# One attention layer on one core: scores and weighings joined into three stretches of TensorE's batch instead of five, products dealt between two PSUM banks, all orders rewritten

## The chip, the core and the metric

The kernel runs on one core of one Trainium2 chip. A core has TensorE (PE in the profile), VectorE (DVE), ScalarE (ACT), GpSimd (POOL) and SyncE (SP), which here issues all DMAs. The metric is the device time of one execution in microseconds (us); lower is better.

## The reference

For 32 batches of 256 rows and 384 columns: attention with 12 heads of 32 columns and an additive bias (`adj`, the same for all heads of a batch), an output product, a residual and a layer norm without gain.

```python
q = (x @ Wq.T).reshape(B, N, NUM_HEADS, HEAD)
k = (x @ Wk.T).reshape(B, N, NUM_HEADS, HEAD)
v = (x @ Wv.T + bv).reshape(B, N, NUM_HEADS, HEAD)
a = jnp.einsum('bnhd,bmhd->bhnm', q, k) * SCALE + encoding_bias[:, None, :, :]
pad_mask = jnp.all(a == 0, axis=-1)
a = jnp.where(pad_mask[..., None], -jnp.inf, a)
a = jax.nn.softmax(a, axis=-1)
o = jnp.einsum('bhnm,bmhd->bnhd', a, v).reshape(B, N, HIDDEN)
return o @ Wo.T + bo
x = _layernorm(x + _L0_gnn_ref(x, adj, ...), axis=-1)
```

## The kernel before

All is float32; products of full width are made of three matmuls of rounded parts (hi x hi, hi x lo, lo x hi). Every engine has its own program, written out by hand as `start()`, then `step(t)` for each of 27 batches (2 to 28), then `end()`. The loop over batches is a Python loop, so the program is unrolled. Engines wait for one another by semaphores; a wait inside an engine's program holds all that stands behind it.

One batch on TensorE. `project_kq` makes K and Q in three products, K01, K2Q0 and Q12, of 18 matmuls each (L779, 256 columns). `project_v` and `project_y` make v and the output in two halves of 9 matmuls each (V0, V1, Y0, Y1; L779, 384 columns). `scores(t, g)`, g = 0, 1, 2, makes the scores of four heads: 24 matmuls on tiles of 32 rows, four side by side (L828), into four banks, which the next group reuses after VectorE has read them. `weigh(t, g)` multiplies the exponentials of four heads with v: 16 matmuls on tiles of 32 columns, four side by side (L869). `transposes(t, u)`, u = 8 to 11, turns the exponentials of group 2 (L839). `spread` turns the inverse sums (L850), and `flag` makes one small product that tells whether a row of scores was all zero.

On VectorE `add_bias(t, u)` (L1185) adds the bias to the scores of two heads for half of the rows and takes their maximum: 12 units u of two heads, four in each group. ScalarE's `exps(t, u)` (L553) takes the exponentials into a ring of four units. The units of groups 0 and 1 are not turned by TensorE: VectorE's `square(t, u)` (L1202) turns their blocks of 32 x 32 into `sq_stage`, SyncE's `store_squares(t, g)` writes that 1 MB to a DRAM tensor (`sq_dram`, L250), and `load_squares(t, g)` reads it back in another order (`sq_probT`, L259). The read waits for the store's landing, and `weigh(t, g)` for the read's. SyncE issues DMAs one by one in its written order; a wait there holds all later ones. `load_bias_sq` and `load_bias` for batch c wait until all `add_bias` up to batch c - 2 are done.

ScalarE copies K and Q out of PSUM (`save_kq`), the turned exponentials (`copy_probT`), the weighed sums (`save_o`), rounds (`split_o_hi`) and normalises (`normalise`). VectorE adds `bv` (`save_v`, L1222), divides (`divide`), adds the residual (`residual`, L1285), takes `moments`, and reads the flag (`read_flag`, `mask`). GpSimd makes the lo parts (`split_xt`, `split_kq`, `split_o_lo`), `widen_inv`, `add_bo` and `deviation`.

PSUM has eight banks: four for scores, `bank_t` for the transposes, and `bank_a`, `bank_b`, `bank_c`. Before a product goes into one of these three, TensorE waits until the one before it in that bank was read, which the program writes as an explicit `pe.wait_ge` on `v_saved`, `kq_saved`, `y_saved`, `o_saved` or `o_n_ready`. Before the change `bank_b` holds K2Q0, Q12, V0, V1, Y0 and Y1, `bank_c` K01 and the spreads, and `bank_a` the weighed sums and the flag.

The order of TensorE in `step(t)` before: T11 of t-1, V1, K01 of t+1, Y0 of t-2, **W1 of t-1, S2**, K2Q0 of t+2, **W2 of t-1**, T8, Y1 of t-2, spread 0, flag, T9, **S0 of t+1**, Q12 of t+2, **W0**, T10, spread 1, V0 of t+1, **S1 of t+1** (W = `weigh`, S = `scores`, T = `transposes`; tiled stretches in bold).

## Time and profile before

| | us |
|---|---|
| median of three runs | 737.46 |
| profiled execution | 735.77 |
| its span, first to last instruction | 733.9 |
| span: start, 27 steps, end | 64.1, 592.4, 77.3 |

| engine | busy us | share of the span |
|---|---|---|
| TensorE, matmuls | 712.3 | 97% |
| TensorE, weight loads | 608.3 | 83% |
| VectorE | 588.5 | 80% |
| ScalarE | 616.7 | 84% |
| GpSimd | 453.0 | 62% |

The span leaves out 1.9 us of the profiled execution. 193 MB move by DMA at a mean of 263 GB/s; TensorE's granted clock is 0.996 of full in the mean. Busy time of TensorE is modelled and overlaps; where the text speaks of a stage's length, it is the time from the stage's first matmul to the next stage's first.

### The profile page before, as it was taken

How to read it: one execution, taken by the hardware profiler on the slowest of the kernel's cores; microseconds unless marked ns; L12 is line 12 of the kernel's file. 1: busy time of each engine (PE TensorE's matmuls, PEld its weight loads, DVE VectorE, ACT ScalarE, POOL GpSimd, SP SyncE). 2: the span in 40 equal slices, each digit the busy share in tenths (PEclk: the TensorE clock that was granted, in tenths of full speed). 3: DMA queues.
4: the chain of work that ended last, by engine and by line, in shares of the span. 5: the costliest groups of instructions: out<-in, count | busy, mean ns of one | idle time of the engine just before them, and what ended most of it. 6: DMA issues, size and time to landing. Idle time of an engine off the chain costs nothing.

```text
span 733.9 us, 23131 instructions
## 1 busy us (share of the span) xinstructions
PE 712.3 (97%) x7567; PEld 608.3 (83%) x7567; DVE 588.5 (80%) x2220; ACT 616.7 (84%) x1993; POOL 453.0 (62%) x516
## 2 busy tenths in 40 slices
PE   7999999999999999999999999999999999999985
PEld 7877888888888888888888888888888888888764
DVE  3886877888887898887798887888887788888873
ACT  4788888888888898888898888898888898888983
POOL 3674566675556675655676566676566676565362
PEclk9999999999999999999999999999999999999999
DMA  8468788878768888778778878878777868877782
GB/s 278 146 231 288 259 267 273 264 258 298 247 251 305 292 253 287 267 238 281 255 262 305 273 262 281 282 249 287 260 280 262 301 234 282 291 264 257 237 317 94
DMA packets 92712, 193.00 MB, mean 263 GB/s; under 512 B 4784, under 2 KB 51632, under 8 KB 84400
## 3 DMA queue, kind: packets, MB, share of 16 engines
q1 hardware_dynamic: 92592, 191.52, 76.9%
q8 instruction: 61, 1.00, 0.5%
q14 instruction: 59, 0.48, 0.2%
HBM read 111.80 MB, written 79.69 MB: 261 GB/s over the span
## 4 chain that ended last, share of the span: by engine, by line
PE 82%; DMA 9%; DVE 3%; POOL 3%; issue 2%; ACT 1%; DVEq 0%; SPq 0%; POOLq 0%; ACTq 0%
PE bank_b L779 41%; PE bank_a L869 11%; PE s_bank L828 10%; PE bank_c L779 8%; PE bank_t L839 8%; DMA sq_dram<-w_f 5%; DMA sq_probT<-sq_dram 3%; PE bank_c L850 2%; POOL kq_lo L400 1%; DVE neg L1185 1%; DVE w_f L1202 1%; DMA xt<-in_xT 0%; POOL kq_hi L398 0%; POOL xt_lo L389 0%; DVEq L1241 0%
## 5 line engine op out<-in xcount | busy, mean ns | idle before, releaser
L553 ACT ACTIVATE prob<-neg,negmax 128x256 f32<-128x256 f32 x768 | 380.6, 501 | 37.1 <-DVE negmax L1185 35.6
L1185 DVE CUSTOM_DVE_ANT_0 neg<-s_bank,bias_sq 128x256 f32<-128x256 f32 x512 | 190.3, 411 | 53.9 <-PE s_bank L828 43.8
L1202 DVE STREAM_TRANSPOSE w_f<-prob 128x512 f32<-128x512 f32 x256 | 173.1, 695 | 0.4 <-ACT prob L553 0.3
L553 ACT ACTIVATION_READ_ACCUMULATOR prob<-neg,negmax 128x1 f32 x768 | 147.8, 192 | 0.0
L400 POOL TENSOR_TENSOR kq_lo<-kq,kq_hi 128x512 fp32r<-128x512 f32 x96 | 125.4, 1306 | 7.7
L779 PE MATMUL bank_b<-xt_hi,w_hi 128*128 128x256 f32 x384 | 115.0, 300 | 0.9 <-POOL xt_lo L389 0.7
L779 PE MATMUL bank_b<-xt_lo,w_hi 128*128 128x256 f32 x384 | 108.6, 283 | 0.0
L779 PE MATMUL bank_b<-xt_hi,w_lo 128*128 128x256 f32 x384 | 108.3, 282 | 0.0
L1185 DVE CUSTOM_DVE_ANT_0 neg<-s_bank,bias 128x256 f32<-128x256 f32 x256 | 92.5, 416 | 10.8 <-PE s_bank L828 10.7
L426 POOL TENSOR_SCALAR var_eps<-meanvar 128x2 f32<-128x2 f32 x32 | 7.3, 228 | 142.7 <-DVE meanvar L1295 142.5
L410 POOL TENSOR_TENSOR o_lo<-o_n,o_hi 128x512 fp32r<-128x512 f32 (+1 forms) x62 | 61.9, 1020 | 38.7 <-ACT o_hi L578 38.6
L839 PE MATMUL bank_t<-ident,prob 128*128 128x128 f32 x512 | 82.9, 284 | 0.5 <-ACT probT L563 0.5
L436 POOL TENSOR_TENSOR xr<-xr,bo_all 128x768 f32<-128x768 f32 x32 | 59.1, 1849 | 38.0 <-DMA xr<-in_x 34.5
L779 PEld LDWEIGHTS bank_b<-xt_hi,w_hi 128*128 128x128 f32 x384 | 73.1, 190 | 8.8 <-DVE v L1222 1.0
L839 PEld LDWEIGHTS bank_t<-ident,prob 128*128 128x128 f32 x512 | 54.4, 141 | 29.2 <-issue 23.5
L563 ACT ACTIVATE probT<-bank_t 128x512 f32<-128x512 f32 x128 | 75.0, 586 | 2.3 <-PE bank_t L839 2.2
L398 POOL CAST kq_hi<-kq 128x512 fp32r<-128x512 f32 x96 | 58.9, 613 | 24.6 <-ACT kq L532 10.4
L779 PEld LDWEIGHTS bank_b<-xt_lo,w_hi 128*128 128x128 f32 x384 | 73.5, 191 | 0.0
L779 PEld LDWEIGHTS bank_b<-xt_hi,w_lo 128*128 128x128 f32 x384 | 73.5, 191 | 0.0
L779 PE MATMUL bank_b<-w_hi,xt_hi 128*128 128x384 f32 x192 | 70.7, 368 | 0.9 <-ACT kq L536 0.7
L869 PE MATMUL bank_a<-sq_probT,v 128*32 128x256 f32 x1008 | 68.3, 389 | 2.5 <-DMA sq_probT<-sq_dram 2.5
L828 PE MATMUL s_bank<-kq_hi 32*128 32x256 f32 x768 | 65.2, 328 | 1.8 <-POOL kq_lo L400 1.6
(83 smaller groups left out, 1779.4 us busy)
## 6 DMA issues: line engine op xcount, KB each, us to landing
sq_dram<-w_f SPq DMA_DIRECT2D x64, 1024.0 KB, 6.3
sq_probT<-sq_dram SPq DMA_DIRECT2D x64, 1024.0 KB, 6.1
xt<-in_xT SPq DMA_DIRECT2D x32, 384.0 KB, 6.0
xr<-in_x SPq DMA_DIRECT2D x32, 384.0 KB, 6.0
out_y<-y_out SPq DMA_DIRECT2D x31, 384.0 KB, 6.7
bias_sq<-in_adjP SPq DMA_DIRECT2D x32, 256.0 KB, 6.4
bias<-in_adj SPq DMA_DIRECT2D x32, 256.0 KB, 6.9
w_f<-in_wkT SPq DMA_DIRECT2D x3, 192.0 KB, 3.9
```

The source lines that it names most:

```text
L398: nc.gpsimd.tensor_copy(kq_hi[t.p][:, a:a + 2, :], kq[:, a:a + 2, :]).then_inc(kq_hi_ready[name], 1)
L400: nc.gpsimd.tensor_tensor(kq_lo[t.p][:, a:a + 2, :], kq[:, a:a + 2, :], kq_hi[t.p][:, a:a + 2, :].bitcast(F32), ALU.subtract).then_inc(kq_ ...
L410: nc.gpsimd.tensor_tensor(o_lo[:, a:b], o_n[:, a:b], o_hi[:, a:b].bitcast(F32), ALU.subtract).then_inc(o_ready, 1)
L436: nc.gpsimd.tensor_tensor(xr[t.p][:], xr[t.p][:], bo_all[:].unsqueeze(1).to_broadcast([P, NT, D]), ALU.add).then_inc(xr_ready, 1)
L553: nc.scalar.activation(prob[:, u % PROB_RING, k], neg[:, h, w.c], ACT.Exp, scale=-1.0, bias=negmax[t.p][:, w.c, h:h + 1], accum_out=sums[t ...
L563: nc.scalar.activation(probT[:, a:a + PAIR, :, P * w.c:P * (w.c + 1)], bank_t[:], ACT.Copy).then_inc(probT_act, 1)
L779: last = nc.tensor.matmul(ps, w_pair[a](k), m_pair[b](k), start=(k == 0 and e == 0), stop=(k == KC - 1 and e == 2))
L828: last = nc.tensor.matmul(s_bank[j][:, c, :], a[t.p][rows, KC + g, P * c:P * (c + 1)], b[t.p][rows, g, :], start=(e == 0), stop=(e == 2))
L839: last = nc.tensor.transpose(bank_t[:, k, m, :], prob[:, u % PROB_RING, k, P * m:P * (m + 1)], ident[:])
L869: last = nc.tensor.matmul(bank_at(t, f"PV{g}")[HD * j:HD * (j + 1), 0:N], v[t.p][:, m, HD * h:HD * (h + 1)], weights, start=(m == 0), stop ...
L1185: nc.vector.tensor_tensor_reduce(out=neg[:, h, w.c], in0=s_bank[h % JH][:, w.c, :], in1=by[t.p][:, w.c, :], scale=-1.0, scalar=BIG, op0=AL ...
L1202: nc.vector.transpose(sq_stage[w.g][:, :, a:a + PAIR, :, w.c].rearrange("p b h m s -> p (h m) b s"), prob[:, u % PROB_RING].rearrange("p k ...
```

## The change

The tiled stretches of a batch are joined: W1, S2 and W2 stand together, and W0 and S1; S0 stays alone. The order of TensorE in `step(t)` becomes K2Q0 and Q12 of t+1, **W1 of t-1, S2, W2 of t-1**, V1, Y0 and Y1 of t-2, T8, flag, **S0 of t+1**, spread 0, T9, V0 of t+1, T10, K01 of t+2, **W0, S1 of t+1**, T11, spread 1. The products are dealt anew to the banks: K2Q0, V0 and Y0 to `bank_b`, K01, Q12, V1 and Y1 to `bank_c`, spreads and weighed sums to `bank_a`. All five engines get new orders in `start`, `step` and `end`. The steps now run over batches 3 to 29, so `start` holds one batch more and `end` one less. On SyncE a step becomes: xt, bias_sq, read of squares 0, store and read of squares 1, out, store of squares 0 of the next batch, xr, bias. No operation is added or removed but for `keep_warm` (9 matmuls less in the start, 7 more in the end).

The core of the diff: the banks, the steps of SyncE, GpSimd, TensorE and VectorE and of ScalarE, the beginnings of the starts and the last part of the ends. The hunks left out reorder the same calls in the same way.

```diff
@@ -141,9 +141,10 @@
     bank_a, bank_b, bank_c = (nc.alloc_psum_tensor(f"bank_{x}", [P, NT * N], F32) for x in "abc")
-    bank = {"PV0": bank_a, "PV1": bank_a, "PV2": bank_a, "K2Q0": bank_b, "Q12": bank_b, "V0": bank_b, "V1": bank_b,
-            "Y0": bank_b, "Y1": bank_b, "K01": bank_c, "R0": bank_c, "R1": bank_c}
+    bank = {"Q12": bank_c, "V1": bank_c, "Y1": bank_c, "K01": bank_c, "PV0": bank_a, "PV1": bank_a,
+            "PV2": bank_a, "R0": bank_a, "R1": bank_a, "K2Q0": bank_b, "V0": bank_b, "Y0": bank_b}
     flags_at = bank_a[:, N:N + NT * H]
 
@@ -294,39 +295,47 @@
                 t4 = Batch(4)
+                load_bias_sq(t1)
                 load_xt(t2)
-                load_xr(t0)
-                load_bias_sq(t1)
+                load_bias(t1)
+                load_xt(t3)
                 store_squares(t0, 0)
-                load_xr(t1)
-                load_xt(t3)
...
             def step(t):
-                nxt3 = t.later(3)
                 nxt2 = t.later(2)
                 nxt = t.later(1)
-                prev2 = t.later(-2)
-                load_bias(nxt)
-                store_squares(t, 0)
-                load_xt(nxt3)
+                prev3 = t.later(-3)
+                load_xt(nxt2)
+                load_bias_sq(nxt2)
                 load_squares(t, 0)
                 store_squares(t, 1)
+                load_squares(t, 1)
+                store_out(prev3)
+                store_squares(nxt, 0)
                 load_xr(t)
-                load_squares(t, 1)
-                load_bias_sq(nxt2)
-                store_out(prev2)
+                load_bias(nxt2)
 
             def end():
@@ -441,38 +441,48 @@
                 t3 = Batch(3)
+                t4 = Batch(4)
+                split_xt(t1)
                 split_kq(t0, "K01")
                 split_kq(t0, "K2Q0")
-                split_xt(t1)
                 split_kq(t0, "Q12")
-                split_kq(t1, "K2Q0")
...
             def step(t):
                 nxt2 = t.later(2)
                 nxt = t.later(1)
                 prev = t.later(-1)
-                prev2 = t.later(-2)
+                prev3 = t.later(-3)
+                deviation(prev3)
+                split_kq(nxt, "K01")
                 widen_inv(prev)
                 split_xt(nxt2)
-                split_kq(nxt, "K2Q0")
-                split_kq(nxt, "Q12")
-                split_kq(nxt, "K01")
-                deviation(prev2)
-                add_bo(t)
+                add_bo(prev)
                 split_o_lo(prev, 0)
+                split_kq(nxt2, "K2Q0")
                 split_o_lo(prev, 1)
+                split_kq(nxt2, "Q12")
 
             def end():
@@ -598,83 +599,109 @@
                 w_hi_part(W_V)
+                w_hi_part(W_O)
+                save_kq(t1, "K2Q0")
                 save_kq(t0, "Q12")
-                w_hi_part(W_O)
                 exps(t0, 0)
                 exps(t0, 1)
                 exps(t0, 2)
...
             def step(t):
-                nxt2 = t.later(2)
                 nxt = t.later(1)
                 prev = t.later(-1)
                 prev2 = t.later(-2)
-                copy_probT(prev, 10)
-                exps(t, 2)
-                split_o_hi(prev2, 0)
-                split_o_hi(prev2, 1)
+                prev3 = t.later(-3)
+                save_kq(nxt, "K01")
                 exps(t, 3)
                 exps(t, 4)
+                save_kq(nxt, "K2Q0")
+                split_o_hi(prev2, 1)
+                copy_probT(prev, 11)
                 exps(t, 5)
-                save_o(prev, 0)
+                save_kq(nxt, "Q12")
+                save_o(prev, 1)
                 exps(t, 6)
-                save_kq(nxt, "K01")
-                save_o(prev, 1)
                 exps(t, 7)
-                copy_probT(prev, 11)
                 exps(t, 8)
-                save_kq(nxt2, "K2Q0")
                 exps(t, 9)
+                normalise(prev3, 0)
                 save_o(prev, 2)
+                normalise(prev3, 1)
+                exps(t, 10)
                 copy_probT(t, 8)
-                exps(t, 10)
                 exps(t, 11)
                 copy_probT(t, 9)
                 exps(nxt, 0)
-                save_kq(nxt2, "Q12")
                 exps(nxt, 1)
-                normalise(prev2, 0)
-                normalise(prev2, 1)
+                copy_probT(t, 10)
+                exps(nxt, 2)
+                split_o_hi(prev, 0)
+                save_o(t, 0)
 
             def end():
@@ -889,73 +890,110 @@
                 t3 = Batch(3)
+                t4 = Batch(4)
                 project_kq(t0, "K01")
                 project_kq(t0, "K2Q0")
-                keep_warm(9)
+                pe.wait_ge(kq_saved["K01"], t0.count(1, 1))
+                project_kq(t0, "Q12")
                 pe.wait_ge(kq_saved["K2Q0"], t0.count(1, 1))
-                project_kq(t0, "Q12")
+                project_kq(t1, "K2Q0")
                 scores(t0, 0)
+                pe.wait_ge(kq_saved["K2Q0"], t1.count(1, 1))
+                project_v(t0, 0)
                 pe.wait_ge(kq_saved["Q12"], t0.count(1, 1))
-                project_v(t0, 0)
-                pe.wait_ge(kq_saved["K01"], t0.count(1, 1))
                 project_kq(t1, "K01")
...
             def step(t):
                 nxt2 = t.later(2)
...
-                transposes(prev, 11)
-
                 pe.wait_ge(v_saved, t.count(NT, 1))
-                project_v(t, 1)
+                project_kq(nxt, "K2Q0")
+
+                pe.wait_ge(kq_saved["K01"], nxt.count(1, 1))
+                project_kq(nxt, "Q12")
 
                 pe.wait_ge(o_n_ready, prev2.count(2, 2))
-                project_kq(nxt, "K01")
-
-                pe.wait_ge(v_saved, t.count(NT, 2))
-                project_y(prev2, 0)
-
-                pe.wait_ge(o_saved[0], prev.count(1, 1))
                 weigh(prev, 1)
                 scores(t, 2)
 
-                pe.wait_ge(y_saved, prev2.count(NT, 1))
-                project_kq(nxt2, "K2Q0")
-
                 pe.wait_ge(o_saved[1], prev.count(1, 1))
                 weigh(prev, 2)
 
+                pe.wait_ge(kq_saved["Q12"], nxt.count(1, 1))
+                project_v(t, 1)
+
+                pe.wait_ge(kq_saved["K2Q0"], nxt.count(1, 1))
+                project_y(prev2, 0)
+
+                pe.wait_ge(v_saved, t.count(NT, 2))
+                project_y(prev2, 1)
+
                 copied(prev, 11)
                 transposes(t, 8)
 
-                pe.wait_ge(kq_saved["K2Q0"], nxt2.count(1, 1))
-                project_y(prev2, 1)
-
-                pe.wait_ge(kq_saved["K01"], nxt.count(1, 1))
-                spread(prev, 0)
-
                 pe.wait_ge(o_saved[2], prev.count(1, 1))
                 flag(t)
+                scores(nxt, 0)
+
+                pe.wait_ge(flag_read, t.count(1, 1))
+                spread(prev, 0)
 
                 copied(t, 8)
                 transposes(t, 9)
-                scores(nxt, 0)
-
-                pe.wait_ge(y_saved, prev2.count(NT, 2))
-                project_kq(nxt2, "Q12")
-
-                pe.wait_ge(flag_read, t.count(1, 1))
-                weigh(t, 0)
+
+                pe.wait_ge(y_saved, prev2.count(NT, 1))
+                project_v(nxt, 0)
 
                 copied(t, 9)
                 transposes(t, 10)
 
+                pe.wait_ge(y_saved, prev2.count(NT, 2))
+                project_kq(nxt2, "K01")
+
                 pe.wait_ge(o_n_ready, prev.count(2, 1))
+                weigh(t, 0)
+                scores(nxt, 1)
+
+                copied(t, 10)
+                transposes(t, 11)
+
+                pe.wait_ge(o_saved[0], t.count(1, 1))
                 spread(prev, 1)
 
-                pe.wait_ge(kq_saved["Q12"], nxt2.count(1, 1))
-                project_v(nxt, 0)
-                scores(nxt, 1)
-
...
 
                 pe.wait_ge(neg_ready, t31.count(H * NT, H * NT))
-                weigh(t31, 1)
-
-                pe.wait_ge(neg_ready, t31.count(H * NT, H * NT))
                 spread(t31, 0)
-                pe.wait_ge(y_saved, t30.count(NT, 1))
-                project_y(t30, 1)
-                pe.wait_ge(o_n_ready, t30.count(2, 2))
-                weigh(t31, 2)
 
                 pe.wait_ge(neg_ready, t31.count(H * NT, H * NT))
                 spread(t31, 1)
-                keep_warm(27)
+                pe.wait_ge(o_n_ready, t30.count(2, 2))
+                weigh(t31, 0)
+                pe.wait_ge(y_saved, t29.count(NT, 2))
+                weigh(t31, 2)
+
+                pe.wait_ge(neg_ready, t31.count(H * NT, H * NT))
+                weigh(t31, 1)
+                pe.wait_ge(y_saved, t29.count(NT, 1))
+                project_y(t30, 0)
+                pe.wait_ge(o_saved[2], t31.count(1, 1))
+                project_y(t30, 1)
+                keep_warm(34)
                 pe.wait_ge(o_n_ready, t31.count(2, 1))
                 project_y(t31, 0)
                 pe.wait_ge(o_n_ready, t31.count(2, 2))
                 project_y(t31, 1)
 
             start()
-            for c in range(2, 29):
+            for c in range(3, 30):
                 step(Batch(c))
             end()
...
             def step(t):
                 nxt = t.later(1)
                 prev = t.later(-1)
                 prev2 = t.later(-2)
-                add_bias(t, 3)
+                prev3 = t.later(-3)
                 square(t, 0)
                 save_v(t, 0)
+                add_bias(t, 4)
                 square(t, 1)
-                add_bias(t, 4)
+                divide(prev2, 1)
                 square(t, 2)
+                square(t, 3)
                 add_bias(t, 5)
-                save_v(t, 1)
-                invert(prev)
                 add_bias(t, 6)
-                square(t, 3)
                 add_bias(t, 7)
-                residual(prev2, 0)
+                moments(prev3, 1)
                 square(t, 4)
                 square(t, 5)
                 add_bias(t, 8)
-                square(t, 6)
-                square(t, 7)
                 add_bias(t, 9)
                 add_bias(t, 10)
+                save_v(t, 1)
                 add_bias(t, 11)
-                moments(prev2, 0)
+                square(t, 6)
                 find_zero(t)
+                square(t, 7)
+                residual(prev2, 0)
+                read_flag(t)
                 residual(prev2, 1)
-                read_flag(t)
                 mask(t)
                 add_bias(nxt, 0)
-                moments(prev2, 1)
                 add_bias(nxt, 1)
+                invert(t)
+                add_bias(nxt, 2)
                 divide(prev, 0)
-                add_bias(nxt, 2)
-                divide(prev, 1)
+                add_bias(nxt, 3)
+                moments(prev2, 0)
 
             def end():
...
                 add_bias(t31, 10)
                 add_bias(t31, 11)
+                find_zero(t31)
+                save_v(t31, 1)
+                read_flag(t31)
                 divide(t30, 0)
-                find_zero(t31)
+                mask(t31)
+                invert(t31)
+                residual(t29, 0)
+                divide(t30, 1)
                 moments(t29, 0)
-                read_flag(t31)
-                divide(t30, 1)
                 residual(t29, 1)
                 moments(t29, 1)
-                mask(t31)
-                invert(t31)
+                divide(t31, 0)
+                divide(t31, 1)
                 residual(t30, 0)
                 moments(t30, 0)
-                divide(t31, 0)
                 residual(t30, 1)
                 moments(t30, 1)
-                divide(t31, 1)
                 split_o_lo(t31, 0)
                 split_o_lo(t31, 1)
```

## Rows read from the trace of the kernel before

**Rows 1.** Stretches: loop, start, end. Busy us (instructions) per engine, clock, DMA share, GB/s.
```profile
64.14:656.56 592.42, 590.88 (x6295) 505.69 (x6291) 487.73 (x1863) 514.21 (x1677) 383.50 (x433) 1.00 0.80 272
0.00:64.14 64.14, 56.65 (x620) 49.91 (x620) 42.76 (x152) 44.74 (x135) 32.20 (x35) 1.00 0.68 226
656.56:733.90 77.34, 64.76 (x661) 52.68 (x657) 57.98 (x206) 57.74 (x184) 37.30 (x49) 0.96 0.65 226
```

**Rows 2.** Waits of PE in the loop: us in total, times, longest.
```profile
PE bank_a L869 <- DMA sq_probT<-sq_dram: 1.2, 3, 0.8
```

**Rows 3.** Timeline of PE: start us, us, line, operation; projection, weighing, transposes.
```profile
360.31 0.28 PE L779 MATMUL bank_b<-xt_lo,w_hi 128*128 128x256 f32 x1
360.43 0.28 PE L779 MATMUL bank_b<-xt_hi,w_lo 128*128 128x256 f32 x1
360.64 1.07 PE L869 MATMUL bank_a<-probT,v 128*32 128x256 f32 x16
361.64 0.66 PE L839 MATMUL bank_t<-ident,prob 128*128 128x128 f32 x4
```

**Rows 4.** Timeline of PE, batch 14: weighing of group 1, scores, projection.
```profile
356.38 1.07 PE L869 MATMUL bank_a<-sq_probT,v 128*32 128x256 f32 x16 [0.30 <-DMA sq_probT<-sq_dram]
357.38 0.39 PE L828 MATMUL s_bank<-kq_hi 32*128 32x256 f32 x4
...
358.30 0.39 PE L779 MATMUL bank_b<-xt_hi,w_hi 128*128 128x256 f32 x1
358.52 0.28 PE L779 MATMUL bank_b<-xt_lo,w_hi 128*128 128x256 f32 x1
358.64 0.28 PE L779 MATMUL bank_b<-xt_hi,w_lo 128*128 128x256 f32 x1
```

**Rows 5.** Timeline of PE, end: scores, then a weighing (its first records).
```profile
662.47 0.39 PE L828 MATMUL s_bank<-kq_hi 32*128 32x256 f32 x4
...
663.38 0.85 PE L869 MATMUL bank_a<-sq_probT,v 128*32 128x256 f32 x12
```

**Rows 6.** Timeline of SyncE, batch 14: start us, time to issue, line, transfer.
```profile
338.79 0.36 SPq L259 DMA_DIRECT2D sq_probT<-sq_dram  x1
...
349.74 0.50 SPq L237 DMA_DIRECT2D bias_sq<-in_adjP  x1
```

**Rows 7.** Chain that ended last, batch 14: start us, us, what.
```profile
339.27 9.96 DMA sq_dram<-w_f
...
349.33 6.91 DMA sq_probT<-sq_dram
```

**Rows 8.** Timelines of PE and DVE: a y of nine matmuls and the addition behind it.
```profile
376.71 0.42 PE L779 MATMUL bank_b<-w_hi,o_hi 128*128 128x384 f32 x1
...
378.57 0.56 DVE L1285 TENSOR_TENSOR y<-bank_b,xr 128x384 f32<-128x384 f32 x1 [1.19 <-PE bank_b L779]
```

**Rows 9.** Timeline of DVE: two score reductions of `add_bias` in a row.
```profile
383.26 0.42 DVE L1185 CUSTOM_DVE_ANT_0 neg<-s_bank,bias 128x256 f32<-128x256 f32 x1
...
383.60 0.42 DVE L1185 CUSTOM_DVE_ANT_0 neg<-s_bank,bias 128x256 f32<-128x256 f32 x1
```

**Rows 10.** Timeline of SyncE, batches 3 and 27: store 0, read 0, read 1.
```profile
91.28 0.33 SPq L250 DMA_DIRECT2D sq_dram<-w_f  x1
...
96.12 0.36 SPq L259 DMA_DIRECT2D sq_probT<-sq_dram  x1
...
105.68 0.36 SPq L259 DMA_DIRECT2D sq_probT<-sq_dram  x1
...
623.12 0.36 SPq L259 DMA_DIRECT2D sq_probT<-sq_dram  x1
...
631.94 0.36 SPq L259 DMA_DIRECT2D sq_probT<-sq_dram  x1
```

**Rows 11.** Tile `sq_probT` in batches 3 to 28: the reads' time to landing.
```profile
DMA to landing us min/median/max: 5.4/6.2/7.2
```

More of the change, by code:

```diff
@@ L509, in _ @@
             start()
-            for c in range(2, 29):
+            for c in range(3, 30):
                 step(Batch(c))
@@ L605, in start @@
                 exps(t0, 2)
+                save_kq(t1, "K01")
                 exps(t0, 3)
-                save_kq(t1, "K2Q0")
                 exps(t0, 4)
                 exps(t0, 5)
-                save_kq(t1, "K01")
                 exps(t0, 6)
@@ L770, in _ @@
             start()
-            for c in range(2, 29):
+            for c in range(3, 30):
                 step(Batch(c))
@@ L942, in start @@
                 transposes(t1, 8)
-                pe.wait_ge(o_n_ready, t0.count(2, 1))
-                spread(t0, 1)
-                pe.wait_ge(kq_saved["K2Q0"], t3.count(1, 1))
-                project_kq(t3, "Q12")
+                pe.wait_ge(kq_saved["Q12"], t2.count(1, 1))
+                project_kq(t3, "K01")
                 pe.wait_ge(o_saved[2], t0.count(1, 1))
@@ L951, in start @@
                 transposes(t1, 9)
-                pe.wait_ge(kq_saved["Q12"], t3.count(1, 1))
-                project_v(t2, 0)
                 pe.wait_ge(flag_read, t1.count(1, 1))
-                weigh(t1, 0)
+                spread(t0, 0)
+                pe.wait_ge(kq_saved["K01"], t3.count(1, 1))
+                project_kq(t3, "Q12")
                 copied(t1, 9)
@@ L1064, in end @@
-                project_v(t30, 1)
-                pe.wait_ge(o_n_ready, t28.count(2, 2))
-                project_kq(t31, "K01")
-                pe.wait_ge(o_saved[0], t29.count(1, 1))
-                weigh(t29, 1)
-                scores(t30, 2)
-                pe.wait_ge(v_saved, t30.count(NT, 2))
+                pe.wait_ge(v_saved, t30.count(NT, 1))
+                project_kq(t31, "K2Q0")
+                pe.wait_ge(kq_saved["K01"], t31.count(1, 1))
+                project_kq(t31, "Q12")
@@ L1146, in _ @@
             start()
-            for c in range(2, 29):
+            for c in range(3, 30):
                 step(Batch(c))
@@ L1308, in start @@
                 w_lo_part(W_V)
+                w_lo_part(W_O)
                 add_bias(t0, 0)
@@ L1517, in _ @@
             start()
-            for c in range(2, 29):
+            for c in range(3, 30):
                 step(Batch(c))
```

522 lines of the change are left out of this document (260 added, 262 removed).

## The prediction

> **What bounds the kernel now.** I read the stretches first, then TensorE's waits, then its timeline in one batch, then the DMA queue. The stretches [rows 1] divide the span into a start of 64.1 us, the 27 unrolled batches of `step` (592.4 us) and an end of 77.3 us. In the loop TensorE is busy 590.9 us of 592.4 at full clock; VectorE has 488, ScalarE 514, GpSimd 384, and the DMA engines are busy 80% of the time. One batch takes 592.42 / 27 = 21.94 us, and that is TensorE's own work: its waits for data in the loop are 1.2 us in three places, all for the read-back of squares [rows 2]. So a batch gets shorter only if TensorE's stages do. In the start and the end TensorE is not the bound: idle for 7.5 us and 12.6 us.
>
> What TensorE spends between stages is in its timeline. Inside a full-array projection matmuls of 256 columns start 0.12 us apart; from the last of K2Q0 to the first of a weighing 0.21 us pass [rows 3]. After scores the first projection matmul starts and the second follows after 0.22 instead of 0.12 us [rows 4]. So entering a stretch of tiled work costs 0.09 us and leaving it 0.10 us. Inside a stretch, a weighing takes 1.00 us to whatever follows, transposes [rows 3] or scores [rows 4], and scores take 0.92 us before a projection [rows 4] and 0.91 before a weighing [rows 5]. A pair thus saves no time of its own, only the way out and back.
>
> **The change, part by part.**
>
> *Stretches.* Before, in a batch: W1+S2, W2, S0, W0, S1 (W for `weigh`, S for `scores`, number = group). After: W1+S2+W2, S0, W0+S1. Two ways in and two ways out fewer: 2 x (0.09 + 0.10) = 0.38, taken as 0.4 us a batch. The same 54 + 36 projections, 16 transposes, 6 spreads and 48 + 72 tiled matmuls remain. 27 x 0.4 = 10.8 us, and TensorE's batch becomes 21.5 us. Bound from below: nothing, if the projections' first matmuls pay anyway; from above 0.5.
>
> The Trainium skill (TensorEngine Tiling, Key Properties) says that a change of tiling mode drains the engine. Scores and weighings are two modes, so by the rule 11 changes a batch become 9, not 10 become 6. Two drains at the 0.2 us of a way out and back are 0.4 us: the same sum, and [rows 4] agrees with it, the weighing being 1.00 us long before scores too.
>
> *Banks.* V0, Y0 and K2Q0 are in bank_b, V1, Y1, Q12 and K01 in bank_c, the spread with the weighings in bank_a. Y0 and Y1 are now adjacent: Y1 waits for `save_v(t, 1)` alone, about 0.9 us ahead of need. W2 needs bank_a emptied by ScalarE's `save_o(1)` during S2's 0.91 us. A weighing's last result is 0.1 us behind its 1.00, the copy takes 0.38, so 0.4 us are left if ScalarE stands ready. It is queued behind `save_kq(Q12)`, which must itself wait for Q12 just before W1, so it should be ready. This costs 0; if ScalarE is inside a pair of exponentials (0.98 us), up to 0.5 us a batch.
>
> *Engine orders.* VectorE's work between two scores stays four `add_bias` and their partners, and the scores now lie almost evenly, some 7.1 us apart; with 18 of 21.5 us busy plus the flag's branch it should keep up: 0. GpSimd: 14.2 of 21.5 us: 0. ScalarE: 19.0 of 21.5: 0, as above.
>
> *The squares' way through memory.* This is where I expect the saving to go. After the last square of group 1 (`square(t, 7)`) the queue stores 1 MB, waits, and reads it back; W1 needs it. Before, from the issue of group 0's read (which precedes that store in the queue) to W1 are 356.38 - 338.79 = 17.6 us for batch 14 [rows 4, 6]. The store came 9.96 us after its issue and the read 6.91 us after its own [rows 7], so that even there W1 waited only 0.3 us. After the change there is less room, because group 0's read moves later against W1. I count from W1's start: W1 1.00, S2 0.91, W2 1.00, so V1 starts at 2.9. VectorE starts on a product of nine matmuls 1.86 us after their start [rows 8], at 4.8; `save_v(t, 1)` 0.5, and only then `add_bias(t, 11)`, two at 0.345 each [rows 9] plus the read of the accumulator 0.08: 6.05. The queue's `load_bias_sq(nxt2)` waits for exactly this one, issues in 0.50 us [rows 6], and behind it stands `load_squares(t, 0)`: 6.6 us after W1's start.
>
> From there: group 0's read to the landing of group 1's store. In 25 batches of the loop it is 8.4 to 10.9 us, mean 9.4: batch 3 has 105.68 - 96.12 = 9.56, batch 27 631.94 - 623.12 = 8.82 [rows 10], batch 14 349.33 - 338.79 = 10.54 [rows 6, 7]. The read that follows takes 5.4 to 7.2 [rows 11], for group 1 6.0 in the mean. With 0.1 for the queue and 0.1 for TensorE, W1 of the next batch starts 6.6 + 9.4 + 0.1 + 6.0 + 0.1 = 22.2 us after W1 of this one. At the quick end it is 6.6 + 8.5 + 0.1 + 5.5 + 0.1 = 20.8, at the slow end 6.6 + 10.5 + 0.1 + 6.9 + 0.1 = 24.2. TensorE's 21.5 lies between. This is a closed loop (W1, W2, V1, `save_v`, `add_bias(11)`, read, store, read, W1), so what is late is not made up. The xr load no longer follows the store closely, which should take some of the slow end off. I take 22.1 us a batch, 0.16 more than before.
>
> That the store waits behind the read is seen in batch 3: the store of group 0, with nothing before it, has landed 4.8 us after its issue (91.28 to 96.12); the other, issued 0.9 us after the read, took 8.6. The Trainium skill (DMA: Bandwidth & Descriptors, Queues, rings and completion order) says that each DMA engine takes a queue's descriptors in ring order; the trace agrees. Were the transfers independent instead, the store would be back in 4.8 us, and the loop above would not bind.
>
> *Start.* TensorE's 7.5 us idle are mostly waits for the first kq splits, for the first weighings' data and for the bank before an o. The new order puts K2Q0 of batch 1 ahead of the first scores, where 1.5 us were idle, and V0 of later batches ahead of waits. Against it `split_xt(t1)` now goes before the first kq splits on GpSimd and `w_hi_part(W_O)` before two copies on ScalarE. I take -4 us (between -6 and +1). *End.* After `square(31, 7)` the store, the read, the last weighing, two divisions, o's split and Y(31) are needed as before; two more residuals stand before the last `split_o_lo` on VectorE (about +1 us), and S0 to S1 of batch 31 is shorter. Taken as 0 (-4 to +4).
>
> **Sum against the profiled execution.** Span 733.9, execution 735.8, median of three runs 737.5 (1.7 above the execution). 735.8 + 27 x 0.16 (4.3) - 4 + 0 = 736.1 us; at the median's level 738.
>
> **Rivals.**
> 1. *The reads land in time.* If the round trip stays near its quick end (batches 19 and 10 of before do), TensorE sets 21.5 us: 735.8 - 27 x 0.44 - 4 = 719.9, at the median's level 722 (716 to 727). For it: half the batches before are under 15 us for the two parts together, and one W1 only in three waited. Against it: room shrinks from 17.6 to 14.8 us, and 16 of 25 batches needed more.
> 2. *The other side: the slow round trip prevails.* As long as it takes 16.4 us or more in the mean (read issue to read landed; before 15.5), the batch is 6.6 + 0.2 + 16.0 or above, 22.8 to 23.2 us: 735.8 + 27 x 1.0 - 4 = 759, at the median's level 760. It passes 2% from 22.6 us a batch on. For it: batch 14 needed 17.5. Against it: the same transfers, less bunched.
> 3. *A wait on ScalarE takes the saving.* `save_o(1)` between W1 and W2 late by 0.4 us a batch, the reads in time: 21.9 us, 735.8 - 1 - 4 = 731, at the median's level 732. For it: only 0.4 us are left. Against it: ScalarE waits for PE just before.
> 4. *The change does nothing to stages:* first matmuls stay slow although stretches are joined, with the DMA as forecast: still 738, since DMA sets the batch.
>
> **How the numbers follow.** Forecast (with 4) 0.52, its own range 730 to 748; rival 1 0.22; rival 3 0.17; rival 2 0.09. About 2% is what a measurement can tell from no change: 722.7 and 752.2. Faster: two thirds of rival 1 and a little of rival 3, 0.17. Slower: rival 2 without its near edge and a little of the forecast, 0.08. Within 2%: 0.75. Range 720 to 750: it leaves out a third of rival 1 and most of rival 2.
>
> **What would show it.** In the loop of after: TensorE idle before W1 (bank_a, `sq_probT`) by 0.5 to 1 us in most batches, busy time down by about 11 us over the loop, W2 directly behind S2 with no wait, V0/Y0/Y1 without gaps; the queue issuing `load_squares(t, 0)` right after `load_bias_sq` some 6.6 us after W1. It would be wrong if W1 hardly waits (rival 1), if idle time stands before W2 (rival 3), or if the start or end moved by more than 6 us.

## The result and the profile after

The changed kernel takes 757.8 us (median of four, 751.9 to 761.7) against 737.1 for the kernel before: a ratio of 1.026, with a 95% interval of 1.022 to 1.030. It is slower by 2.6%. Ratios and intervals are worked out from the executions in the chip's faster state, not from the medians, and one execution of the kernel before and one of e4, of 1353 us each, count in no ratio and in no range. The prediction said 738 us, with 720 to 750 as its range: it was wrong, and the time is close to the 760 us of its second rival. The profiled execution took 754.9 us, its span is 753.0.

First the stretches, here in the order start, loop, end, with the columns of [rows 1].

```profile
0.00:78.08 78.08, 75.05 (x829) 66.91 (x830) 61.31 (x219) 64.02 (x199) 43.30 (x47) 1.00 0.72 248
78.08:694.30 616.22, 587.39 (x6295) 513.74 (x6293) 497.88 (x1866) 519.77 (x1675) 381.96 (x432) 0.99 0.76 260
694.30:753.00 58.70, 45.12 (x448) 36.48 (x446) 40.74 (x137) 38.48 (x120) 25.04 (x37) 0.95 0.65 226
```

The loop of 27 batches takes 616.2 us in place of 592.4: 22.82 us a batch in place of 21.94. Start and end together take 136.8 in place of 141.5, 4.7 less. So 735.8 - 4.7 + 23.8 = 754.9: all of the loss is in the loop. There TensorE is busy 587.4 us of 616.2, where it had been busy 590.9 of 592.4; the DMA engines are busy less of the time (0.76 for 0.80).

TensorE's longest waits, whole span, and below them its only wait inside the loop (us in total, times, longest):

```profile
PE bank_a L870 <- DMA sq_probT<-sq_dram: 32.7, 21, 2.9
PE bank_t L840 <- ACT probT L564: 1.7, 3, 0.8
...
PE bank_a L870 <- DMA sq_probT<-sq_dram: 28.6, 18, 2.7
```

The chain that ended last, from the page, shares of the span by engine (PE 47% and DMA 40%; in e1 below they are 87% and 5%):

```profile
PE 47%; DMA 40%; DVE 7%; issue 4%; ACT 1%; POOL 0%; SPq 0%; DVEq 0%; ACTq 0%; POOLq 0%
```

In the loop TensorE is idle for 28.8 us, and 28.6 of them are the wait for the read-back of squares, which before was 1.2 us in three places [rows 2]. One turn of the loop shows where it comes from. SyncE's timeline, from the read of group 0 of batch 13 to the store of group 1 of batch 14:

```profile
314.91 0.37 SPq L238 DMA_DIRECT2D bias_sq<-in_adjP  x1
315.40 0.40 SPq L260 DMA_DIRECT2D sq_probT<-sq_dram  x1
316.90 0.34 SPq L251 DMA_DIRECT2D sq_dram<-w_f  x1
325.75 0.36 SPq L260 DMA_DIRECT2D sq_probT<-sq_dram  x1
...
340.61 0.37 SPq L238 DMA_DIRECT2D bias_sq<-in_adjP  x1
341.10 0.40 SPq L260 DMA_DIRECT2D sq_probT<-sq_dram  x1
343.19 0.34 SPq L251 DMA_DIRECT2D sq_dram<-w_f  x1
```

VectorE's timeline, what `load_bias_sq` at 314.91 waited for:

```profile
313.64 0.56 DVE L1222 TENSOR_TENSOR v<-bank_c,bv_all 128x384 f32<-128x384 f32 x1 [0.41 <-PE bank_c L780]
314.12 0.41 DVE L1185 CUSTOM_DVE_ANT_0 neg<-s_bank,bias 128x256 f32<-128x256 f32 x1
...
314.46 0.42 DVE L1185 CUSTOM_DVE_ANT_0 neg<-s_bank,bias 128x256 f32<-128x256 f32 x1
314.80 0.08 DVE L1185 DVE_READ_ACCUMULATOR2_ANT negmax<- 128x1 f32 x1
```

TensorE's timeline around W1 of two batches, each followed by S2, W2 and the first product of V1:

```profile
308.86 1.07 PE L870 MATMUL bank_a<-sq_probT,v 128*32 128x256 f32 x16 [1.14 <-DMA sq_probT<-sq_dram]
309.86 0.39 PE L829 MATMUL s_bank<-kq_hi 32*128 32x256 f32 x4
...
310.77 1.07 PE L870 MATMUL bank_a<-probT,v 128*32 128x256 f32 x16
311.77 0.44 PE L780 MATMUL bank_c<-w_hi,xt_hi 128*128 128x384 f32 x1
...
330.06 0.28 PE L780 MATMUL bank_c<-xt_hi,w_lo 128*128 128x256 f32 x1
333.04 1.07 PE L870 MATMUL bank_a<-sq_probT,v 128*32 128x256 f32 x16 [2.70 <-DMA sq_probT<-sq_dram]
334.04 0.50 PE L829 MATMUL s_bank<-kq_hi 32*128 32x256 f32 x4
...
335.53 1.94 PE L870 MATMUL bank_a<-probT,v 128*32 128x256 f32 x16
337.40 0.52 PE L780 MATMUL bank_c<-w_hi,xt_hi 128*128 128x384 f32 x1
```

Read them together. W1 starts at 308.86, V1 at 311.77, VectorE starts `save_v(t, 1)` at 313.64 and has the last `add_bias` done at 314.88. Only then does SyncE get past `load_bias_sq`, and the read of group 0 goes out at 315.40, 6.54 us after W1, although its data had been ready for 3.2 us (the store of group 0 had landed at 312.2). The store of group 1 behind it has landed by 325.7, the read at 325.75 takes until 332.9 (7.15 us, one of six long reads, see e7), and W1 of the next batch starts at 333.04, 24.2 us after the one before. TensorE sat idle for the 2.70 us that stand in W1's row.

VectorE's timeline holds one thing more, the last `add_bias` of the same batch that reads `bias_sq`:

```profile
307.38 0.42 DVE L1185 CUSTOM_DVE_ANT_0 neg<-s_bank,bias_sq 128x256 f32<-128x256 f32 x1
```

The units of group 2, from 311.07 on, read `bias`. So the buffer that `load_bias_sq` fills was free at 307.8, ahead of W1, and the wait in SyncE, which asks for all twelve units, lasts 7.1 us longer than the data need. By these times a wait for unit 7 alone would have opened the gate before the read's data were there. No run tries it.

The last lines of TensorE's timeline hold a second loss. After that idle time S2 and W2 take 3.36 us (334.04 to 337.40); in the turn before they took 1.91 (309.86 to 311.77). The granted clock of the two stretches (columns: stretch, its length, TensorE's busy time, clock, DMA share, GB/s):

```profile
334.10:337.30 3.20, 3.20 (x42) 0.51 0.98 353
309.90:311.70 1.80, 1.80 (x43) 1.00 0.96 380
```

At half the clock (1.2 in place of 2.4 GHz) V1 starts 1.5 us later, so the gate of the next turn opens 1.5 us later too: 341.10 is 8.06 us after 333.04. The section "HAM oscillation" of the Trainium skill (TensorE: Matmul & The Clock Gate) describes this, a wait on a DMA that makes the work behind it start at the low clock. The trace agrees in kind, in 5 of 26 turns: the waits in the example of the Trainium skill are 3 to 5 us long, the five here 1.85 to 2.73 us.

What the 1.5 us do to the turn is not always the same. In four of the five turns that follow, the next W1 did not wait at all: TensorE's own work, part of it at the low clock, took 22.95 to 22.97 us in place of 21.41 and was the longer path. In the fifth (24.89 us) the late gate set the turn, with 1.85 us of waiting at its end. In the second profile of after (e7) it was the late gate in all three such turns inside the loop (24.92, 25.18 and 24.29 us).

### The profile page after: what moved, and what is told of

Its sections match the earlier page's. It is cut to its first block, busy times and chain, and to the rows that moved or that the text cites. A ratio compares the mean times of both kernels' runs of the same rounds, so it can differ in the third digit from the quotient of the medians.

```text
span 753.0 us, 23127 instructions
## 1 busy us (share of the span) xinstructions
PE 707.6 (94%) x7565; PEld 617.1 (82%) x7565; DVE 599.9 (80%) x2220; ACT 622.3 (83%) x1993; POOL 450.3 (60%) x516
## 4 chain that ended last, share of the span: by engine, by line
PE 47%; DMA 40%; DVE 7%; issue 4%; ACT 1%; POOL 0%; SPq 0%; DVEq 0%; ACTq 0%; POOLq 0%
DMA sq_dram<-w_f 22%; DMA sq_probT<-sq_dram 17%; PE bank_c L780 17%; PE bank_a L870 11%; PE bank_b L780 8%; PE s_bank L829 7%; PE bank_t L840 3%; DVE w_f L1202 2%; DVE neg L1185 2%; PE bank_a L851 1%; DVE zero_max L1228 1%; DVE w_lo L1170 1%; DMA xt<-in_xT 0%; DVE negmax L1185 0%; DVE v L1222 0%
## 5 line engine op out<-in xcount | busy, mean ns | idle before, releaser
L780 PE MATMUL bank_c<-xt_hi,w_hi 128*128 128x256 f32 x384 | 111.5, 290 | 0.5 <-DVE w_lo L1164 0.5
L780 PE MATMUL bank_c<-xt_lo,w_hi 128*128 128x256 f32 x384 | 108.5, 282 | 0.0
L780 PE MATMUL bank_c<-xt_hi,w_lo 128*128 128x256 f32 x384 | 108.2, 282 | 0.0
L571 ACT ACTIVATE o_raw<-bank_a 128x256 f32<-128x256 f32 x94 | 35.6, 378 | 62.4 <-PE bank_a L870 62.1
L780 PEld LDWEIGHTS bank_c<-xt_hi,w_hi 128*128 128x128 f32 x384 | 73.4, 191 | 1.3 <-issue 1.2
L780 PEld LDWEIGHTS bank_c<-xt_lo,w_hi 128*128 128x128 f32 x384 | 73.5, 191 | 0.0
L780 PEld LDWEIGHTS bank_c<-xt_hi,w_lo 128*128 128x128 f32 x384 | 73.3, 191 | 0.0
L870 PEld LDWEIGHTS bank_a<-sq_probT,v 128*32 128x32 f32 x1008 | 28.8, 110 | 52.4 <-issue 38.3
L840 PEld LDWEIGHTS bank_t<-ident,prob 128*128 128x128 f32 x512 | 59.6, 140 | 9.6 <-ACT probT L564 2.4
L829 PEld LDWEIGHTS s_bank<-kq_hi 32*128 32x128 f32 x768 | 38.5, 189 | 31.0 <-issue 27.1
```

What stands on the lines that cost most here:

```text
L571: nc.scalar.activation(o_raw[t.p][:, g, :], bank_at(t, f"PV{g}")[:, 0:N], ACT.Copy).then_inc(o_saved[g], 1)
L780: last = nc.tensor.matmul(ps, w_pair[a](k), m_pair[b](k), start=(k == 0 and e == 0), stop=(k == KC - 1 and e == 2))
L829: last = nc.tensor.matmul(s_bank[j][:, c, :], a[t.p][rows, KC + g, P * c:P * (c + 1)], b[t.p][rows, g, :], start=(e == 0), stop=(e == 2))
L840: last = nc.tensor.transpose(bank_t[:, k, m, :], prob[:, u % PROB_RING, k, P * m:P * (m + 1)], ident[:])
L870: last = nc.tensor.matmul(bank_at(t, f"PV{g}")[HD * j:HD * (j + 1), 0:N], v[t.p][:, m, HD * h:HD * (h + 1)], weights, start=(m == 0), stop ...
```

## Experiments

The table has the means over the 26 turns from W1 of batch 3 to W1 of batch 29 in each profile. "Gate" is W1 to the issue of the next read of group 0, "store" that issue to the landing of the store of group 1, "read" the issue of the read of group 1 to its landing, "rest" what remains until W1 (0.14 where TensorE stood waiting) with 0.1 for the queue. The four make up the turn. In the rows of after: 6.84 + 9.40 + 6.38 + 0.32 = 22.94. In the kernel before the last two of the 26 turns reach into its end; the 24 within its loop have a mean of 21.92 us.

| kernel | gate | store | read | rest | turn | time, us (median) |
|---|---|---|---|---|---|---|
| before | 3.98 | 9.34 | 5.97 | 2.50 | 21.78 | 737 to 739 |
| after | 6.84 | 9.40 | 6.38 | 0.32 | 22.93 | 757.8 |
| after again (e7) | 6.77 | 9.53 | 6.25 | 0.31 | 22.86 | 758.5 |
| gate gone (e1) | 3.50 | 9.20 | 6.12 | 2.62 | 21.44 | 718.5 |
| gate's wait only (e2) | 6.19 | 8.81 | 6.29 | 0.53 | 21.81 | 731.9 |
| filler (e3) | 6.65 | 9.74 | 6.10 | 0.47 | 22.96 | 757.4 |
| third buffer (e5) | 3.45 | 9.79 | 5.76 | 2.43 | 21.44 | 718.9 |
| `save_v` later (e6) | 5.60 | 9.58 | 6.06 | 0.86 | 22.09 | 735.5 |

### e1: the gate taken away

```diff
                 load_xt(nxt2)
-                load_bias_sq(nxt2)
                 load_squares(t, 0)
                 store_squares(t, 1)
                 load_squares(t, 1)
+                load_bias_sq(nxt2)
                 store_out(prev3)
```

> The kernel after with one line of SyncE's step moved: load_bias_sq(nxt2) goes from ahead of load_squares(t, 0) to behind load_squares(t, 1). In the profile of after the read of group 0 is issued 6.54 us after W1 (8.07 in the batches whose W1 was latest), although the store before it had landed some 3.1 us earlier; read issue to landing of store 1 is 9.4 us, the read of group 1 6.4 us. Theory (the gate closes the loop W1, V1, save_v, add_bias(11), read 0, store 1, read 1, W1): without it the read of group 0 goes 3 us earlier, W1 no longer waits, and TensorE's own 21.4 us set the batch: span 78.1 + 27 x 21.4 + 58.7 = 714.6, time 716 us (712 to 722), TensorE at full clock in the loop. Rival (the transfers themselves are too slow or too many, the DMA engines being busy 74% of the span): the store of group 1 lands as late as before, W1 goes on waiting by over 1 us a batch, and the time stays above 745 us.

Measured: 718.5 us, ratio 0.972 to the kernel before (0.966 to 0.979). The same turn of SyncE (W1 was at 298.41):

```profile
301.70 0.37 SPq L260 DMA_DIRECT2D sq_probT<-sq_dram  x1
306.10 0.34 SPq L251 DMA_DIRECT2D sq_dram<-w_f  x1
311.70 0.36 SPq L260 DMA_DIRECT2D sq_probT<-sq_dram  x1
312.11 0.50 SPq L238 DMA_DIRECT2D bias_sq<-in_adjP  x1
```

and the stretch of its loop (columns as in [rows 1]):

```profile
79.71:657.85 578.14, 578.08 (x6295) 508.01 (x6293) 495.29 (x1866) 519.14 (x1675) 381.91 (x432) 1.00 0.81 278
```

TensorE is busy 578.08 of 578.14 us at full clock, 578.14 / 27 = 21.41 us a batch. DMA carries the same bytes in less time (0.81 busy). The rival, transfers too slow or too many, falls. One line in SyncE's order was worth 39 us, and without it the change is a gain of 2.7% over the kernel before.

The traces show what the earlier read does. The store of group 1 is issued at about the same time after W1 in both kernels, 8.04 us in after and 7.68 in e1 (means), for it waits for VectorE's squares. But in after it takes 8.2 us to land and in e1 5.0, because the read of group 0 is by then mostly out of its way: in after, e1, e2, e5 and e6 alike the store lands 2.6 to 2.9 us behind that read (means).

### e2 and e5: the gate's two halves, its wait and its transfer

e2 keeps the wait and moves the transfer; e5 keeps the transfer and takes the wait away, through a third buffer for `bias_sq` in the part of `w_f` that the squares leave free.

```diff
-                load_bias_sq(nxt2)
+                after(sp, neg_ready, nxt2.count(H * NT, -H * NT))
                 load_squares(t, 0)
                 store_squares(t, 1)
                 load_squares(t, 1)
+                load_bias_sq(nxt2)
```

Of e5 the core; the semaphores and the reads of the third buffer are left out.

```diff
+    bias_sq.append(w_space[:, AREA * SQUARED:AREA * SQUARED + NT * N].rearrange("p (c n) -> p c n", c=NT))
...
-                after(sp, neg_ready, t.count(H * NT, -H * NT))
-                sp.dma_start(bias_sq[t.p][:], adjP[t.c].rearrange("(c p) m -> p c m", p=P)
+                after(sp, neg_ready, t.count(H * NT, -2 * H * NT))
...
+                sp.dma_start(bias_sq[t.c % 3][:], adjP[t.c].rearrange("(c p) m -> p c m", p=P)
```

> As e1, but SyncE still waits for the last add_bias of the batch ahead of load_squares(t, 0); only the transfer of bias_sq (256 KB) goes behind load_squares(t, 1). Theory (it is the wait that costs): the read of group 0 is issued 0.5 us earlier than in after, at 6.0 us after W1, and the batch goes from 22.9 to about 22.4 us; time 742 to 752 us. Rival (it is the 256 KB in the queues ahead of the read): about as quick as e1, under 725 us.

> The kernel after with SyncE's order unchanged, bias_sq still transferred ahead of load_squares(t, 0), but into a third buffer, so that load_bias_sq(nxt2) waits for the last add_bias of the batch before, long past. It is the other half of e2, which kept the wait and moved the transfer (731.9 us, batch 21.8). Theory (the wait is what makes the loop; the 256 KB are 0.6 us within it and nothing outside): the read of group 0 goes as soon as its store has landed, 3.4 us after W1, TensorE sets 21.4 us, time 716 to 722 us. Rival (the transfer ahead of read and store costs by itself): over 725 us.

Measured: e2 731.9 us (ratio 0.992, 0.988 to 0.995), between the two forecasts; e5 718.9 us (0.973, 0.966 to 0.981), as the theory said. With the wait kept and the transfer moved (e2) 26 of the 39 us come back, with the transfer kept and the wait gone (e5) all of them, so the two halves do not add up. In e2 the read of group 0 goes out at 6.13 us in nearly every turn, and from there to the landing of the store it takes 8.81 us, 0.59 less than in after. In e5, where only the transfer is back, that part is 9.79, 0.59 more than in e1. So 256 KB ahead of read and store cost 0.6 us in the queues, twice measured (by the spread of the turns give or take 0.2), besides 0.4 for their issue. Where they go behind the read of group 1 instead, that read is longer: 6.12 us in e1, 5.76 in e5. I had expected 22.4 us for e2's turn because I had left those 0.6 us out; with them the loop has come so close to TensorE's 21.41 that most turns are in time. The wait is what makes the loop; the transfer lengthens it. Both fit the ring order that the prediction cited from the Trainium skill (DMA: Bandwidth & Descriptors, Queues, rings and completion order).

### e6: a dose of the gate

```diff
                 add_bias(t, 10)
-                save_v(t, 1)
                 add_bias(t, 11)
+                save_v(t, 1)
                 square(t, 6)
```

> The kernel after with save_v(t, 1) on VectorE behind add_bias(t, 11) in place of ahead of it. The last add_bias then needs no v: it ends about 0.9 us earlier (0.5 for save_v and 0.4 in which VectorE waited for V1), and the gate in SyncE opens as much earlier, 5.6 us after W1. Theory (the loop is closed, each of its terms counts in full in every late batch): the read of group 0 at 5.6 to 5.7 us after W1, the batch 22.1 to 22.4 us in place of 22.9, time 737 to 747 us. Rival (the batch is set by how much the DMA queues carry): 752 us or more as in after.

Measured: 735.5 us, the median of 724.9, 735.0, 736.0 and 739.7, with a wide interval (ratio 0.976 to 1.001), so at the forecast's lower edge or below it (737 to 747), and surely below after. SyncE's timeline; W1 was at 279.61:

```profile
284.70 0.37 SPq L238 DMA_DIRECT2D bias_sq<-in_adjP  x1
285.19 0.40 SPq L260 DMA_DIRECT2D sq_probT<-sq_dram  x1
```

The gate opens at 5.58 us as expected, 0.96 earlier, and the turn is 22.09 us, 0.84 shorter than in after. With e1, e2 and e6 the turn follows the sum of its terms down to TensorE's 21.41 and no further. The rival, a batch set by how much the queues carry, falls a second time.

### e4: the same gate put into the kernel before

```diff
                 load_xt(nxt3)
+                load_bias_sq(nxt2)
                 load_squares(t, 0)
                 store_squares(t, 1)
                 load_xr(t)
                 load_squares(t, 1)
-                load_bias_sq(nxt2)
```

> The kernel before with one line of SyncE's step moved: load_bias_sq(nxt2) goes from behind load_squares(t, 1) to ahead of load_squares(t, 0), as in after; banks, TensorE's and all other orders stay as they were. In before the last add_bias of batch 14 ends 6.3 us after W1, while the read of group 0 was issued on average 4.0 us after W1. Theory (gate): the read is issued 6.8 us after W1 in every batch, and with 9.3 for the store, 6.0 to 6.4 for the read and 0.2 between them the loop is 22.3 to 22.7 us in place of 21.85; time 748 to 762 us, TensorE idle before W1. Rival (the new banks and orders of TensorE, VectorE or ScalarE are what made after slow): 737 to 741 us, as before.

Measured: 803 us (median of 801, 803 and 812; ratio 1.092, 1.081 to 1.103). The rival falls: with every bank and every other order of before, this line alone costs 9%. But my number was too small by over 40 us, and the reason is worth seeing. TensorE's weighings of the squares in the kernel before (W1 of batch 11, W0 of batch 12):

```profile
289.84 1.07 PE L869 MATMUL bank_a<-sq_probT,v 128*32 128x256 f32 x16
...
301.47 1.07 PE L869 MATMUL bank_a<-sq_probT,v 128*32 128x256 f32 x16
```

and in e4 (W1 of batch 11, W0 and W1 of batch 12):

```profile
313.54 1.07 PE L869 MATMUL bank_a<-sq_probT,v 128*32 128x256 f32 x16
...
326.91 1.07 PE L869 MATMUL bank_a<-sq_probT,v 128*32 128x256 f32 x16 [1.67 <-DMA sq_probT<-sq_dram]
...
337.13 1.07 PE L869 MATMUL bank_a<-sq_probT,v 128*32 128x256 f32 x16
```

SyncE's timeline of that turn of e4, the reads of group 0 and 1:

```profile
320.32 0.40 SPq L259 DMA_DIRECT2D sq_probT<-sq_dram  x1
...
329.36 0.36 SPq L259 DMA_DIRECT2D sq_probT<-sq_dram  x1
```

The read of group 0 goes out 6.78 us after W1, as expected. But what it delays is not W1. In the order of before W0 stands 11.63 us after W1; the read needs 6.78 + 6.45 + 0.14 = 13.37, so W0 is late, and 10.22 us of TensorE's own work lie between W0 and the next W1: 13.37 + 10.22 = 23.59 us a turn. That is the turn when all else is in time; the mean over its loop is 657.29 / 27 = 24.34. The rest comes from turns in which W0 waited 2.1 to 3.9 us, some of them with the low clock behind it. Here the read of group 1 lands 1.9 us before it is needed. I had followed only the loop through W1. In after W0 stands 14.4 us after W1, and the same read is in time by 1.4 us in most turns: the change's TensorE order had made room for W0 and taken it from W1.

### e3: less idle time at the low clock

```diff
                 pe.wait_ge(o_n_ready, prev2.count(2, 2))
+                for _ in range(10):
+                    nc.tensor.matmul(bank_a[:, 0:P], ones[:], ones[:], start=True, stop=True)
                 weigh(prev, 1)
                 scores(t, 2)
```

> The kernel after with ten small products of ones (0.055 us each, as the 34 at its end) on TensorE between Q12 and W1 of each batch of the loop, so that TensorE is idle 0.55 us less where W1 waits. In after, in five or six of 26 batches in which W1 waited 2.1 to 3.0 us, the granted clock of what follows is half, the scores and the weighing behind W1 take 3.4 us in place of 1.9, and the next read of group 0 is issued 8.07 instead of 6.54 us after W1. Theory (the lost clock is a part of the loop of its own, some 0.3 us a batch): more work and no more time, 748 to 757 us, with the read of group 0 at 6.54 us in all or nearly all batches. Rival (the clock does nothing, the waits alone count): the batches that were in time become 0.5 us longer and the late ones stay, 760 us or more.

Measured: 757.4 us, no different from after. In the trace the gate is 6.54 us in 25 of 26 turns and 9.34 in the one whose W1 had waited 3.6 us; in after five were at 8.1. So the lost clock did go, but for that turn. In the turns that are in time the ten products cost what they take: 22.0 us in place of 21.41. The time can't tell the theories apart: the store part was slower in this trace (9.74), and the spread of the runs (756 to 764) is as large as the gain looked for. That the low clock costs 5 x 1.5 / 26 = 0.3 us a turn rests on the rows of after, not on this run.

### e7 and e8: after once more, and one stretch taken apart again

e7 is the kernel after, unchanged. e8 is e1 with `weigh(prev, 2)` behind `project_v(t, 1)`, so that W2 is a tiled stretch of its own again.

```diff
-                pe.wait_ge(o_saved[1], prev.count(1, 1))
-                weigh(prev, 2)
                 pe.wait_ge(kq_saved["Q12"], nxt.count(1, 1))
                 project_v(t, 1)
+                pe.wait_ge(o_saved[1], prev.count(1, 1))
+                weigh(prev, 2)
```

> The kernel after once more, unchanged, for a second trace of its loop beside e5 and e6. In the first, per batch: gate 6.84 us after W1 (6.54, and 8.07 behind the latest W1), 9.40 from read 0 to store 1, 6.38 for read 1, together 22.93. Expected: 6.5 to 6.9, 9.2 to 9.8, 6.0 to 6.5; time 752 to 762 us. Rival (the first trace was a slow one by chance in its reads): reads at 6.0 and the batch at 22.4, time 745.

> The kernel e1 (gate gone, 718.5 us, TensorE sets 21.41 us a batch) with W2 taken out of the joined stretch again: TensorE's order is W1, S2, V1, W2, Y0, Y1 in place of W1, S2, W2, V1, Y0, Y1. Theory (a tiled stretch costs 0.09 us to enter and 0.10 to leave): 21.60 us a batch, 5 us more, 723 to 725 us. Rival (the 0.44 us that e1's batch is shorter than the one of before have another source, as the banks): 718 to 719 us as e1.

Measured: e7 758.5 us, its terms in the table within 0.15 us of the first trace. Single reads of group 1 of 7 to 8.6 us appear in both (six of 26 in the first, two in the second; in the loop of before none of group 1 was over 6.91). e8 725.4 us, 0.4 above the forecast's range; the stretch of its loop:

```profile
78.43:663.25 584.82, 583.81 (x6295) 507.03 (x6293) 504.76 (x1866) 518.71 (x1675) 382.18 (x432) 1.00 0.79 275
```

Nearly every turn is 21.62 us, 0.21 more than e1's 21.41 (584.82 / 27 = 21.66 holds one late turn besides). One more tiled stretch costs 0.21 us, and the rival (another source for the saving) falls. This agrees with the rule of the Trainium skill that the prediction cited (TensorEngine Tiling (Array Packing), Key Properties), and puts a price on it for this kernel; twice 0.21 is 0.42 of the 0.44 us by which e1's turn is shorter than the commonest of before.

## Why the prediction was wrong, point by point

**What bounded before, and what the stretches save: right.** Forecast 21.5 us for TensorE's batch, and 0.4 from two stretches. e1, e5 and the quick turns of after run at 21.41; the commonest turn of before is 21.85; e8 gives 0.21 a stretch.

**Banks and engine orders at nothing: right.** W2 starts right behind S2 (309.86 to 310.77 is 0.91 us), no wait stands before V0, Y0 or Y1, and e1 holds TensorE busy throughout with all of them in place. So rival 3 (a wait on ScalarE before W2) did not come, nor rival 4.

**Start and end: right.** Forecast -4 together, measured -4.7. By the rows of both profiles TensorE's idle time fell from 7.5 to 3.0 us in the start (forecast -4) and rose from 12.6 to 13.6 in the end (forecast 0); the other 1.2 us are work.

**The squares' loop: the right mechanism, the wrong size, and this is the step that failed.** The loop through W1, V1, `save_v`, `add_bias(11)`, read, store, read was named, with its gate at 6.6 us (measured 6.54) and 9.4 us from read to store (measured 9.40). What failed is the sum for the turn, 6.6 + 9.4 + 0.1 + 6.0 + 0.1 = 22.2, lowered to 22.1: it came out at 22.93, because its read was 0.4 us too short and it put the low clock at nothing. Over the loop's 27 batches (22.82 in the mean against 22.1) this is the 20 us between forecast and result. The parts of the 0.83:
- the read of group 1: 6.0 forecast, 6.38 measured (6.25 in e7), a few single reads of 7 to 8.4 us making up the difference: 0.38;
- the clock, which the sum did not have: five gates of 8.1 us in place of 6.54: 0.3, less 0.06 by which the gate itself was shorter;
- the rest, 0.32 in place of 0.2: 0.12. I added up means, where each turn takes the larger of two, the transfers' way and TensorE's. Most of it (0.08) comes from the three low-clock turns in which the transfers were clearly early and TensorE's slowed work of 22.95 us was the longer, the remainder from turns at its 21.41;
- the 0.1 that I took off because xr no longer follows the store.

Within the 9.40 two errors hid each other. The 256 KB of `bias_sq` ahead of the read cost 0.6 us, by e2 and e5, and I had counted only their issue; something else was quicker than in before: without these 256 KB ahead the part takes 8.81 us in e2 and 9.20 in e1, against 9.34. It may be xr's new place, but no run separates that.

**The chances.** Rival 2, 22.8 to 23.2 us a turn and 760 us, has the number and was given 0.09. But its condition was a round trip, from the issue of read 0 to the landing of read 1, of 16.4 us or more, and that did not come: it was 15.86 in after and 15.87 in e7, against 15.4 before. The rival's 22.8 takes 16.0 for it, less than its own 16.4, and a longer gate (6.84 for 6.6) and rest (0.32 for 0.2) filled the difference. So its number was partly luck. I put "the same transfers, less bunched" against it and left out what the loop does to itself when it is late: a late W1 can cost clock, and lost clock makes the next W1 later. The sum of the terms was within 0.4 us of the 2% line of 22.6; a range to 750 was too narrow for that, since a turn can come out longer by any of its terms, but never shorter than TensorE's 21.4.

**The signs.** Waits before W1 in most turns: yes, 1.1 us in the mean (0.5 to 1 was forecast). Busy time down by 11 us over the loop: only by 3.5, since five turns at the low clock put some 7.5 back.

**Three readings of the rows were off.** In the 25 batches of before the part from read 0 to the landing of store 1 was 8.1 to 10.9 us, not 8.4 to 10.9 (the mean, 9.4, is right). Of them 11 had both parts together under 15 us, not half, and 16 needed over 14.8. Of the 27 W1 of the loop two waited, those of batches 1 and 14, not one in three. None of this changes the sum.

**What stays open.** What makes single reads take 7 to 8.6 us is not settled. Nor is the share of the clock measured by a run of its own, nor was a wait for unit 7 alone tried.

The version that beats both kernels is e1: the change with `load_bias_sq(nxt2)` behind `load_squares(t, 1)`, 718.5 us; e5 is as fast, at the price of a third buffer.

## What to carry to other kernels

In a queue that works in order, a load that must wait for a buffer holds up everything behind it: write beside each issue what it waits for and until when, ask whether the wait names the buffer's last reader or a later one, and put a transfer that is needed a batch later behind the ones that are needed now. Here that one line was worth 39 us, and some 65 in the old kernel. Where a round trip closes a loop, follow every consumer of it (W0 as well as W1), take the larger of the two for each turn and not for the means, and count the bytes that stand ahead as well as their issue.

## What the hardware showed that was not expected

- TensorE's clock fell to half behind single waits of some 2 to 3 us in the middle of full work: after 2.70 us of idle time S2 and W2 took 3.36 us in place of 1.91. Of the seven idle times before W1 of 1.85 us or more in the loop of after, five were followed by it (1.85, 2.40, 2.67, 2.70 and 2.73) and two were not (2.35 and 2.41); in e7 it was four of eight, and in e4 one of 3.54 us was not. The length of the one wait does not settle it. What it costs is 1.5 us on the next turn.
- 256 KB ahead of a read and a store of 1 MB each lengthen the pair by 0.59 us, in both directions of the test (8.81 and 9.40; 9.20 and 9.79).
- The store of group 1 lands 2.6 to 3.1 us behind the read of group 0 in the mean of every profile, whether it was issued 0.7 us after that read (e4), 1.2 (after) or 4.2 (e1, e5). So it takes 8 to 9 us where it follows closely and 5.0 to 5.6 where the read had 4 us to itself.
- Reads of group 1, 1 MB each and mostly 5.6 to 6.6 us long, took 7.0 to 8.6 us now and then: six times in the profile of after, two in each of e6, e7 and e8, one in e3 and e4, never in before, e1, e2 and e5.
